# Attention-result stores moved from GpSimd's stream to SyncE's, ahead of its loads

## The reference

```python
x = L0_attn_x
x = _layernorm(x + _L0_attn_ref(x, w_qkv, w_out))        # causal softmax attention, 16 heads of 8
x = _layernorm(x + _L0_ffn_ref(x, ...))                  # ternary-weight gated MLP, hidden 512
x = _layernorm(x + _L1_attn_ref(x, Wq, Wk, Wv, Wo))      # rotary linear attention with decay
x = _layernorm(x + _L1_ffn_ref(x, W_gate, W_in, ...))    # mixture of 8 experts, top 2
```

```python
scores = jnp.einsum('bhqd,bhkd->bhqk', q, k) * scale
scores = jnp.where(causal[None, None, :, :], scores, -jnp.inf)
weights = jax.nn.softmax(scores, axis=-1)
out = jnp.einsum('bhqk,bhkd->bhqd', weights, v)
```

## Time and profile before

| | |
|---|---|
| time, median of 3 runs | 1447.83 us (1446.66 to 1451.39) |
| the profiled execution's own time | 1454.15 us |
| its span, first to last instruction | 1452.5 us |
| busy over the span | PE 86%, DVE 66%, ACT 45%, POOL 41% |
| POOL's 248 store issues (L1492) | 124 x 504 ns and 124 x 511 ns, 126.0 us in all |
| the softmax attention stage | about 80 to 560 us, 16 units of some 30 us |

### The profile page before, as it was taken

The page is one execution under the profiler, slowest core; times in us unless marked ns, Lnnn a source line. Parts: engine busy times, 40 slices in busy tenths (PEclk is TensorE's granted clock), DMA queues, the critical chain, the costliest instruction groups (busy, mean ns, idle before and its releaser), DMA issues. The chain is left out here.

```text
span 1452.5 us, 45404 instructions
## 1 busy us (share of the span) xinstructions
PE 1249.5 (86%) x16752; PEld 764.2 (53%) x16753; DVE 963.2 (66%) x2007; ACT 657.3 (45%) x1312; POOL 598.5 (41%) x739
## 2 busy tenths in 40 slices
PE   6689999999999974999999999999999967399990
PEld 4244444444444431356565665657465635299980
DVE  6867777777777842257675858585867556466656
ACT  4156666666666663242524333342424231155553
POOL 7123544435444452024352616162534344254456
PEclk9589999999999996999999999999999988599995
DMA  6452112121121104030312213130403050322215
GB/s 192 117 185 59 46 46 58 49 57 46 46 61 49 54 14 131 11 97 2 96 26 64 57 38 83 34 87 22 105 7 87 8 152 2 88 88 66 62 57 174
DMA packets 100079, 98.88 MB, mean 68 GB/s; under 512 B 19952, under 2 KB 84336, under 8 KB 99824
## 3 DMA queue, kind: packets, MB, share of 16 engines
q1 hardware_dynamic: 78096, 77.01, 18.6%
q0 software_dynamic: 13152, 15.43, 4.1%
q10 hardware_dynamic: 8704, 4.59, 1.1%
HBM read 51.94 MB, written 24.72 MB: 53 GB/s over the span
## 5 line engine op out<-in xcount | busy, mean ns | idle before, releaser
L1393 DVE TENSOR_REDUCE arena<-banks 128x4 f32<-128x512 f32 (+3 forms) x336 | 345.1, 1068 | 94.9 <-PE banks L1202 90.0
L1334 ACT ACTIVATE arena<-banks 128x512 f32<-128x512 f32 x576 | 304.9, 603 | 197.4 <-PE banks L1202 194.1
L1202 PE MATMUL banks<-arena 99*32 99x512 bf16 (+7 forms) x6144 | 342.8, 335 | 29.6 <-ACT arena L1334 11.4
L1202 PEld LDWEIGHTS banks<-arena 96*32 96x32 bf16 (+1 forms) x6144 | 150.9, 97 | 194.6 <-ACT arena L1334 69.7
L423 PE MATMUL banks<-arena,h 128*128 128x512 f32 x512 | 226.7, 593 | 2.4 <-DVEq L368 1.0
L1483 POOL TENSOR_SCALAR_AFFINE_SELECT arena<-arena 128x512 f32<-128x512 f32 x128 | 80.1, 639 | 250.1 <-ACT arena L1334 249.4
L1269 PE MATMUL banks<-arena 128*32 128x512 f32 (+3 forms) x1536 | 154.0, 491 | 23.7 <-POOL arena L1483 23.6
L423 PEld LDWEIGHTS banks<-arena,h 128*128 128x128 f32 x512 | 94.7, 190 | 110.0 <-issue 105.7
L439 POOL TENSOR_TENSOR arena<-arena 128x4 f32<-128x4 f32 x24 | 24.5, 1019 | 282.3 <-DVE arena L437 282.3
L571 ACT ACTIVATE arena<-banks,sh 128x512 f32<-128x512 f32 x64 | 44.0, 688 | 212.6 <-PE banks L423 212.6
L610 POOL TENSOR_TENSOR arena<-arena,qdec 128x512 f32<-128x512 f32 x64 | 87.7, 1392 | 62.7 <-DVE arena L514 41.8
(11 more groups left out here) (160 smaller groups left out, 1934.9 us busy)
## 6 DMA issues: line engine op xcount, KB each, us to landing
arena<-arena SPq DMA_DIRECT2D x160, 128.0 KB
arena<-k_parts SPq DMA_DIRECT2D x96, 96.0 KB
arena<-rows SPq DMA_DIRECT2D x72, 65.0 KB
arena<-q_parts SPq DMA_DIRECT2D x64, 64.0 KB
arena<-best SPq DMA_DIRECT2D x16, 256.0 KB, 4.5
k_parts<-arena SPq DMA_DIRECT2D x24, 128.0 KB, 3.1
arena<-q_parts SPq DMA_DIRECT2D x32, 96.0 KB
q_parts<-arena POOLq DMA_DIRECT2D x18, 128.0 KB, 2.9
```

The costliest lines, as they stand in the source:

```text
L1202: ins = nc.tensor.matmul(dst[c:c + 32, :], lhs[:, c:c + 32], rhs, start=start, stop=stop, skip_group_check=True)
L1334: nc.scalar.activation(pe_[:, s % NSLOT, :], score[s % NBANK], ACT.Exp, scale=SCALE0)\
L1393: nc.vector.tensor_reduce(mx[:, 1 if k0 else 0, qt, hs[0]:hs[-1] + 1], src, AX.X, ALU.max)\
```

## The change

The 8 stores of a half are issued by SP, in a new function `weighted`, at the beginning of SP's unit: first qc = 1 of the unit before, then qc = 0 of this unit, both ahead of the wait for step 26 and of the loads of unit u + 2. They wait for the same `s_ta` and raise the same `s_att` as before. POOL keeps its triangles and `lay_v`.

```diff
@@ SP
+            def weighted(v, qc):
+                e.wait_ge(s_ta, QC * v + qc + 1)
+                for h in range(HQ):
+                    for to, at in ((att_t, 32 * h), (att_s, 32 * h + D0)):
+                        e.dma_start(to[v, h, :, qc * 512:(qc + 1) * 512], ta[at:at + D0, qc, :])\
+                            .then_inc(s_att[qc], 16)
+
             def unit(u, p, first, last, i):
                 more = not (isinstance(u, int) and u >= NU - 2)
+                if not first:
+                    weighted(u - 1, 1)
+                weighted(u, 0)
                 if more:
                     e.wait_ge(s_qk, NS * u + FIRST_STEP[HALF_GROUP])
                     stacks(u + 2, p, 0)
@@ POOL
             def unit(u, p, first, last, i):
-                def store(v, qc):
-                    e.wait_ge(s_ta, QC * v + qc + 1)
-                    for h in range(HQ):
-                        for to, at in ((att_t, 32 * h), (att_s, 32 * h + D0)):
-                            e.dma_start(to[v, h, :, qc * 512:(qc + 1) * 512], ta[at:at + D0, qc, :])\
-                                .then_inc(s_att[qc], 16)
                 for g in range(NG):
                     if g in DIAGONAL:
                         triangle(u, g)
-                    if g == 1 and not first:
-                        store(u - 1, 1)
-                    if g == 5:
-                        store(u, 0)
-                        if not first and not last:
-                            lay_v(u + 1, 1 - p)
+                    if g == 5 and not first and not last:
+                        lay_v(u + 1, 1 - p)
```

## The result

| | before | after |
|---|---|---|
| median of the runs beside each other | 1449.18 us (1446.66 to 1451.39, 4 runs) | 1430.4 us (1428.9 to 1431.48, 4 runs) |
| ratio | | 0.987, 95% interval 0.985 to 0.9891 |
| span of the profiled execution | 1452.5 us | 1429.7 us |
| first of ACT's last stores, where the attention stage ends | 559.25 us | 542.08 us |

The kernel is 18.8 us faster by the medians; the interval of the ratio allows 15.8 to 21.7 us. In the two profiled executions the attention stage ends 559.25 - 542.08 = 17.2 us earlier. Their spans differ by more, 22.8 us: the other 5.6 us lie behind the stage, and the profiled execution of before was a long one (1454.15 us against its median of 1449.18).

A forecast was written before the change was run, and what follows sets the result against it. PE was taken to bound the attention stage, waiting for POOL's group 2 select behind eight stores. Of 15.4 to 17.4 us, 16.5 was taken, with nothing added: 1447.83 - 16.5 = 1431.3 us, range 1426 to 1441 us.

The forecast's parts named there:

- What bounds the stage: Attention stage: PE, busy 91%, sets the pace; its largest wait is 23.6 us for POOL's triangles, 15.1 us before 256-column matmuls.
- The select of group 2 was late by POOL's queue alone: POOL: eight stores delay the select to 483.01; its exponentials are ready at 479.81, so without the block the wait vanishes.
- The price of a regular unit: PE at group 2's `times_v`: each regular unit loses 1.04 us, 0.89 us idle plus 0.15 us of lost overlap.
- The sum of 17.4 us: Attention stage, upper bound of the gain: 15.1 us of waits in 15 units plus 2.3 us of lost overlap.
- unit 15: PE's wait before group 2 in this unit: 2.21 us idle, counted as 2.36 us, with no maxima left.
- How much comes through: ACT and DVE behind PE: 1.22 and 0.90 us idle let the gain through; 15.4 to 17.4 us, taken as 16.5.
- What is added: SP: 16 store issues a unit, 4.1 us a block, hidden in holes of its stream; cost 0.
- the slack of 2.4 to 2.7 us: Behind SP's second block: 2.7 us before PE needs the loads of unit u + 2, 2.4 us for the maxima's transfers.
- Rivals 1 and 2: Attention stage: DVE nearly saturated, half lost, 1440 us, chance 0.11; stall moves to another wait, 1447.8 us, chance 0.06.
- Rival 3: SP: dear issues, above 0.99 us each, make the maxima late; slower, 1472 us at 1.35 us an issue, chance 0.05.
- Rival 4: POOL, free sooner, also shortens waits before the 384-column matmuls, up to 8 us more gain, 1423 us; chance 0.04.
- the 8.5 us: PE's wait for POOL's triangles before the 384-column matmuls, groups 1 and 8; predicted to stay.

The follow-up runs named there:

- e1: Changed kernel, but only the qc = 1 block goes to SP; POOL keeps the qc = 0 block after group 2: 1432.47 us, ratio 0.9873 to before.
- e3: Kernel before, with POOL's qc = 1 block issued after group 2's triangle instead of ahead of it, nothing on SP: 1432.64 us, ratio 0.9887 to before.
- e2: Changed kernel, but only the qc = 0 block goes to SP; POOL keeps qc = 1 between the triangles of groups 1 and 2: 1451.23 us, ratio 1.0005.
- e5: The changed kernel run again, unaltered, for comparison: 1430.03 us, ratio 0.9869 to before.
- e6: Changed kernel with each SP store issued twice, the second copy to spare DRAM tensors, 16 issues a block: 1430.58 us, ratio 0.9881 to before.
- e4: Changed kernel with each SP store issued three times, further copies to spare DRAM tensors, 24 issues a block: 1497.15 us, ratio 1.0332 to before.
- e7: Changed kernel with POOL signalling after each of the two selects of groups 1 and 8, PE waiting for each separately: 1426.39 us, ratio 0.984 to before.

## Why the prediction was right

- **What bounds the stage: right.** PE's idle time for POOL ahead of group 2, and what hangs on it, was what the change took away. From 120 to 530 us PE is now busy 385.8 us instead of 374.6 us.
- **The select of group 2 was late by POOL's queue alone: right.** e1 and e3 have the whole gain, e2 none of it. It starts 0.16 us after ACT's step 9 (468.93 to 469.09), in e3 too; I had said within 0.1 us.
- **The price of a regular unit, 1.04 us: right.** It is 1.07 us by the trace (30.03 to 28.96), where the idle time alone gave 0.89. The idle time in the rows understates what a late matmul costs.
- **The sum of 17.4 us: too small by one term, unit 15.** That it comes so near the 17.2 us by which the stage ended earlier is luck. From the select of group 1 of unit 1 to that of unit 14, 13 units with a stall, before takes 507.87 - 116.17 = 391.70 us and the changed kernel 495.92 - 119.05 = 376.87 us, 14.8 us less, where the terms of the prediction give 12 x 1.04 + 1.35 = 13.8; 0.8 us of it is a single wait for `arena<-q_parts` that only the trace of before has. From there to ACT's last stores it is 51.38 and 46.16 us, 5.2 us less, where the terms give 1.04 + 2.36 = 3.4. Together 20.0 us, 19.2 without that single wait, and the stop in unit 0 hides 2.8 of the 20.0. I had put unit 15 at 2.36 us, its idle time and the overlap. From its group 1 (535.87 before, 522.83 after) to ACT's last stores it gives 4.13 us, because behind the 2.21 us of idle time the clock fell, which a window that ends at 530 us does not show. The same 216 matmuls, in before and in the changed kernel:

```profile
535.87:559.25 23.38, 16.97 (x216) 5.70 (x216) 0.00 (x0) 15.42 (x30) 12.29 (x23) 0.85 0.07 13
```

```profile
522.83:542.08 19.25, 14.71 (x216) 5.18 (x216) 0.00 (x0) 15.21 (x30) 4.28 (x7) 1.00 0.07 13
```

PE works 2.3 us longer in before, and it is idle 1.9 us longer. It is not an accident of one execution: the stretch from the select of group 1 of unit 14 to ACT's last stores is 50.96 us in e2, whose block stands where it stood before, and 46.15 to 46.18 us in e1, e3, e5 and e6.
- **How much comes through: all of it, where I took 16.5 us out of 15.4 to 17.4.** DVE gave its gap of 0.90 us, and 0.07 us of the next (0.55 to 0.48); ACT had 1.22. The 18.8 us of the medians are more than the 17.4 of the upper end, and the 1.8 us that unit 15 gave beyond its term are about that difference; the uncertainty of the ratio, some 3 us either way, is larger than it.
- **What is added, nothing: right, at a lower price.** A store costs SP 0.40 us with its addresses (3.2 us a block) where I allowed 0.51. e6 shows that twice that is still hidden, by the slack of 2.4 to 2.7 us behind the hole and not by the hole alone.
- **Rivals 1 and 2** (DVE takes half back, or all goes to another wait) are contradicted by the unit of 28.96 us. **Rival 3** (SP's issues late) has its place but not its price: e4 shows the mechanism, at 24 issues a block, with PE waiting for the loads first. I had named the maxima as the deciding wait, and counted neither the first block's overflow nor the clock. **Rival 4** did not occur; the 8.5 us needed e7.
- **The rule weighed.** The Trainium skill, page "DMA: Bandwidth & Descriptors", section "Issuing engines are not separate DMA queues", says that another issuer saves only the sequencer's time, usually small beside the transfer. For one store the trace of before agrees: its issue holds POOL for 0.50 us, and its landing comes 1.8 us after it in the median. Read as a forecast of no gain it was wrong here, since eight issues stood between two steps of PE's chain. But e3 supports its substance: who issues does not matter, only what stands behind the issues.

## What to carry to other kernels

Look at what stands in an engine's queue between a result being ready and the instruction that hands it on. Eight DMA issues of 0.5 us were no load for POOL, 41% busy, but they stood ahead of a 0.65 us select that PE waited for. Before an issue block is moved to another engine, try it one place later on its own: here a single number did the same.

Where a block is moved, find the hole that it goes into, its length and what is late next, and count blocks that overflow into one another: at twice the issues the cost was nothing that could be measured, at three times 67 us.

When a sum and a profile agree, look whether the parts agree too. Here a short term (unit 15) and an accident of the profiled execution (unit 0) nearly cancelled.

## What the runs showed of the hardware

The same 16 KB store holds POOL for 504 to 511 ns in the median, ACT's queue for 281 to 724 ns and SP's for 276 ns in the median (one took 1447 ns), 0.40 us with a loop's address instructions and 0.33 us without them, in unit 1 (125.83 to 128.46, eight stores). The rows of the changed kernel on `att_t` (ns min/median/max, first and last start):

```profile
L1163 SPq DMA_DIRECT2D att_t<-arena x124: 275/276/321, 96.5 to 530.5; - x124
...
L1361 ACTq DMA_DIRECT2D att_t<-arena x4: 281/458/724, 542.1 to 544.7; - x4
```

How long SP's stores take to land the trace does not say; it gives no such time for them.

A stop of PE can cost more than itself, because the granted clock falls to half behind it. How long the stop is does not settle that alone, as these stops show:

- e4, a wait of 4.8 us: about 4 us at 0.50 behind it, the unit 7.2 us longer.
- e4, waits of 3.01 us (at 447.33 and 276.49): the clock stays at 1.00, the units are 2.7 us longer. The row behind the first of them is below. A wait of 2.91 us (at 549.15) is followed by 0.50 in the same run.
- before, unit 15, a wait of 2.21 us, 2.4 us after one of 1.32 us ended: 0.50 from 542 to 546.
- the changed kernel, unit 0, 1.87 us: 0.50 from 94 to 96. In e3 a stop of 1.92 us at the same place leaves the clock at 1.00.
- before, the waits of 0.89 us of the regular units: 1.00.

```profile
448.00:452.00 4.00, 4.00 (x116) 2.42 (x112) 3.44 (x5) 2.06 (x4) 0.00 (x0) 1.00 0.31 92
```
